# Second routed experts: gate and up of an expert as one load, rows laid out by partition

## The reference, cut to what matters

```python
# hidden_states: [4, 512, 512] -> x: [2048, 512]; w13: [8, 704, 512]; w2: [8, 512, 352]
probs = jax.nn.softmax(router_logits.astype(jnp.float32), axis=-1)
routing_weights, selected_experts = jax.lax.top_k(probs, TOP_K)      # TOP_K = 2
combined = jnp.zeros(x.shape, dtype=jnp.float32)
for e in range(E):                                                   # E = 8
    w_e = jnp.where(selected_experts == e, routing_weights, 0.0).sum(-1)
    h = _silu_and_mul(x @ w13[e].T) @ w2[e].T    # gate: first 352 columns, up: last 352
    combined = combined + w_e[:, None] * h.astype(jnp.float32)
out = shared + combined.astype(x.dtype)
```

## Time and profile before

| what | us |
|---|---|
| runs | 2451.46 median of 3 (2451.32 to 2454.49) |
| profiled execution, its own time | 2455.11 |
| its span in the profile | 2453.5 |
| busy: TensorE | 1960.5 (80%) |
| busy: VectorE | 1437.5 (59%) |
| busy: GpSimd | 1038.2 (42%) |
| busy: ScalarE | 896.1 (37%) |
| mean granted clock of TensorE, share of full speed | 0.917 |

### The profile page before, as it was taken

One profiled execution on the slowest core, in us unless ns is written; L12 is line 12 of the kernel. 1 busy time (PEld: TensorE's weight loads), 2 busy tenths in 40 slices (PEclk: granted clock), 3 DMA queues, 4 the chain that ended last, 5 costly groups with the idle time before them and its releaser, 6 DMA issues. The chain is left out here.

```text
span 2453.5 us, 22106 instructions
## 1 busy us (share of the span) xinstructions
PE 1960.5 (80%) x5587; PEld 956.0 (39%) x5587; DVE 1437.5 (59%) x2046; ACT 896.1 (37%) x1461; POOL 1038.2 (42%) x944
## 2 busy tenths in 40 slices
PE   7367786886886648888888873999999998989990
PEld 2122332332343213333333332666666654555550
DVE  5699888888962649999899975333332331111113
ACT  4455454555521345666466630111111111222220
POOL 0377666666730228888788862010000050000005
PEclk9588898899988769999999996999999999999995
DMA  6403012021001654655747435010000038888886
GB/s 219 191 0 137 1 43 113 0 85 70 5 13 62 239 203 154 241 212 182 262 158 296 167 115 212 20 43 9 26 9 9 9 146 290 301 302 307 298 275 214
DMA packets 159159, 345.77 MB, mean 141 GB/s; under 512 B 14944, under 2 KB 54880, under 8 KB 150368
## 3 DMA queue, kind: packets, MB, share of 16 engines
q1 hardware_dynamic: 146992, 305.23, 34.7%
q0 software_dynamic: 12080, 39.59, 4.7%
HBM read 286.06 MB, written 58.72 MB: 141 GB/s over the span
## 5 line engine op out<-in xcount | busy, mean ns | idle before, releaser
L541 POOL TENSOR_TENSOR work<-work,big 128x512 f32<-128x512 f32 x512 | 658.9, 1295 | 194.2 <-DVE bank L594 188.5
L594 DVE TENSOR_TENSOR_SCAN bank<-bank,work 128x512 f32<-128x512 f32 x512 | 624.8, 1221 | 114.8 <-ACT bank L502 55.3
L437 PE MATMUL bank<-work,ident 128*128 128x512 f32 x896 | 507.7, 678 | 210.1 <-DVE work L570 181.4
L502 ACT ACTIVATE bank<-work,An 128x512 f32<-128x512 f32 x512 | 349.3, 690 | 377.1 <-DVE work L570 373.9
L437 PEld LDWEIGHTS bank<-work,ident 128*128 128x128 f32 x896 | 162.4, 205 | 501.9 <-DVE work L570 356.5
L570 DVE TENSOR_TENSOR work<-bank,big 128x512 f32<-128x512 f32 x512 | 343.9, 672 | 4.3 <-PE bank L437 4.2
L1065 PE MATMUL bank<-big,work 128*128 128x352 f32 x1024 | 315.7, 462 | 4.0 <-DMA big<-sdown 3.3
L1065 PEld LDWEIGHTS bank<-big,work 128*128 128x128 f32 x1024 | 191.7, 191 | 105.4 <-issue 6.1
L1581 PE MATMUL bank<-W,work 128*128 128x512 f32 x384 | 193.7, 617 | 2.1 <-ACT work L1657 1.2
L696 DVE SCALAR_TENSOR_TENSOR work<-work,bank 128x352 f32<-128x352 f32 x39 | 20.3, 521 | 272.8 <-ACT work L691 272.8
L1040 PE MATMUL bank<-big,W 128*128 128x512 f32 x352 | 157.0, 595 | 0.6 <-ACT W L983 0.6
(11 more groups left out here) (270 smaller groups left out, 2363.3 us busy)
## 6 DMA issues: line engine op xcount, KB each, us to landing
big<-bc_d SPq DMA_DIRECT2D x64, 1024.0 KB, 6.7
W<-gate SPq DMA_DIRECT2D x24, 1024.0 KB, 5.3
W<-up SPq DMA_DIRECT2D x24, 1024.0 KB, 5.2
W<-down SPq DMA_DIRECT2D x24, 1024.0 KB, 5.6
work<-xs_d SPq DMA_DIRECT2D x63, 256.0 KB, 5.2
W<-gate SPq DMA_DIRECT2D x20, 704.0 KB, 6.3
W<-up SPq DMA_DIRECT2D x20, 704.0 KB, 7.6
Y<-gate SPq DMA_DIRECT2D x19, 704.0 KB, 6.2
```

The costliest lines, as they stand in the source:

```text
L437: nc.tensor.matmul(YS[:, :], ident[:, :], hC[ring[u[0]]], start=v == 0, stop=v == sums - 1).then_inc(sum_done, 1)
L502: nc.scalar.activation(H[i % 4][:, :], delta[j % 2], ACT.Exp, scale=An[:, j, i:i + 1]).then_inc(dA_done, 1)
L541: nc.gpsimd.tensor_tensor(dBu[i % 2], du[j % 2], Bb[:, i, :], ALU.mult).then_inc(dBu_done, 1)
L594: nc.vector.tensor_tensor_scan(H[i % 4][:, :], H[i % 4][:, :], dBu[i % 2], 0.0, ALU.mult, ALU.add).then_inc(scan_done, 1)
```

## The change

On the host, the transposed `w13` (512 rows of 704 floats per expert: gate, then up) is laid out by partition: for partition p the four rows c * 128 + p stand one behind the other, 2816 floats. The first 256 rows of down are laid out the same way (1024 floats a partition), and the last 96 rows become an array of their own. In the kernel, one DMA brings gate and up of a tile (128 x 2816 floats, 11264 bytes per partition in one piece, where each of the two loads had pieces of 352 floats, 1408 bytes), and one brings the first two blocks of down (pieces of 4096 bytes for 2048). What stands where in SBUF is the same as before, and so are the instructions of all other engines. SyncE's wait for the gate matmuls of tile t - 2 falls away; the merged load waits for the up matmuls of tile t - 2. TensorE's waits ahead of gate and ahead of up now both name the merged load's semaphore.

```diff
--- before.py
+++ after.py
@@ -1296,14 +1296,15 @@
             S["y_out"] = [sem(f"e{k}_y_out{q}") for q in range(2)]
             S["hT_part"] = sem(f"e{k}_hT_part")
             S["xn_in"] = [sem(f"e{k}_xn_in{q}") for q in range(2)]
-            wsem = {m: [sem(f"e{k}_{m}_in{q}") for q in range(2)] for m in ("g", "u", "d")}
+            wsem = {m: [sem(f"e{k}_{m}_in{q}") for q in range(2)] for m in ("gu", "d")}
             WS = [wset(k, q) for q in range(2)]
+            flat = [W, Y[:, :, :].rearrange("p t l -> p (t l)")]
             sh_in, sh_added = sem(f"e{k}_shared_in"), sem(f"e{k}_shared_added")
             shared = wk(9)
 
             def w_in(t, q, done):
-                m = done[0]
-                per = {"g": 16, "u": 16, "d": 32}[m]
+                m = "d" if done[0] == "d" else "gu"
+                per = {"gu": 16, "d": 32}[m]
                 return wsem[m][q], (t - q) * (per // 2) + per
 
             S["w_in"] = w_in
@@ -1317,14 +1318,11 @@
                         if not is_last(t, N):
                             at_least(sp, S["xtr_done"], t)
                             sp.dma_start(xn[1 - q], xs_v[t + 1]).then_inc(S["xn_in"][1 - q], 16)
-                        at_least(sp, S["g_done"], t - 1)
-                        sp.dma_start(WS[q][0], w["gate"][e].rearrange("(c p) f -> p c f", p=P)).then_inc(wsem["g"][q], 16)
                         at_least(sp, S["u_done"], t - 1)
-                        sp.dma_start(WS[q][1], w["up"][e].rearrange("(c p) f -> p c f", p=P)).then_inc(wsem["u"][q], 16)
+                        sp.dma_start(flat[q][:, 0:DK * 2 * F], w["gate_up"][e]).then_inc(wsem["gu"][q], 16)
                         at_least(sp, S["d_done"], t - 1)
-                        dv = w["down"][e]
-                        sp.dma_start(WS[q][2][:, 0:full, :], dv[0:full * P, :].rearrange("(c p) n -> p c n", p=P)).then_inc(wsem["d"][q], 16)
-                        sp.dma_start(WS[q][2][0:F - full * P, full, :], dv[full * P:F, :]).then_inc(wsem["d"][q], 16)
+                        sp.dma_start(flat[q][:, DK * 2 * F:DK * 2 * F + full * D], w["down"][e]).then_inc(wsem["d"][q], 16)
+                        sp.dma_start(WS[q][2][0:F - full * P, full, :], w["down_last"][e]).then_inc(wsem["d"][q], 16)
 
                     def load_shared(i):
 
@@ -1916,10 +1914,16 @@
     }
     w13 = a["L1_ffn_w13"].transpose(0, 2, 1)
     F = w13.shape[2] // 2
+    w2 = a["L1_ffn_w2"].transpose(0, 2, 1)
+
+    def by_partition(v):
+        e, r, f = v.shape
+        return v.reshape(e, r // 128, 128, f).transpose(0, 2, 1, 3).reshape(e, 128, -1)
+
     moe1 = {
         "router": give("router1", np.concatenate([a["L1_ffn_gate_w"], a["L1_ffn_shared_gate_w"]]).T),
-        "gate": give("gate1", w13[:, :, :F]), "up": give("up1", w13[:, :, F:]),
-        "down": give("down1", a["L1_ffn_w2"].transpose(0, 2, 1)),
+        "gate_up": give("gate_up1", by_partition(w13)),
+        "down": give("down1", by_partition(w2[:, :256])), "down_last": give("down_last1", w2[:, 256:]),
         "shared_gate_up": give("sgu1", a["L1_ffn_shared_gate_up_w"].T),
         "shared_down": give("sdown1", a["L1_ffn_shared_down_w"].T),
     }
```

## The result

The changed kernel takes 2482.78 us in the median (2480.19 to 2483.54, 4 runs) against 2452.97 for the kernel before (4 runs). The ratio is 1.0119, 95% interval 1.0101 to 1.0136: 1.2% slower, 29.8 us by the medians. The forecast was 0.7% and 2468.0, with 2480 as the upper end. The sign was right, the size was not.

A forecast was written before the change was run, and what follows sets the result against it. TensorE was taken to set the pace, with loads just in time. Cadence 12.4, scatter 2.0 and start 2.1 us summed to 16.5 us, giving 2468.0 us, 0.7% slower, range 2454 to 2480.

The forecast's parts named there:

- That the merge makes TensorE wait, and the sign: Gate matmuls would wait for the whole merged load, in most tiles, making the kernel 0.7% slower.
- L: Time from a burst's beginning to the landing of the load the gate matmuls wait for: 10.12 us after the change.
- The slower cadence: Bursts of loads would overlap less as tiles take longer, taking 0.2 us off the landing time.
- the rows alone: Longer rows of gate and up would move faster, saving 0.38 us per tile's load (bounds 0.16 and 0.61).
- The landing: The merged load would land 7.4 us after its issue (6.8 to 8.0 by the bounds).
- The start: Tile 0's gate matmuls would start 2.1 us later, waiting for up's landing, with nothing to hide it.
- the cadence: Time per tile in the changed stage would rise from 9.216 to 9.56 us, 12.4 us over 36 tiles.
- Scatter: Single late landings in the changed stage, left out by medians, would add 2 us (bounds 0 and 4).
- the prediction's loop: Two tiles take burst to landing, plus 0.12 us to gate start, plus 8.88 to the next burst but one.
- The first: Rival: long rows save nothing and bursts don't relieve each other, 9.85 us a tile, 2479 us; chance 0.15.
- The second: Rival: row saving and burst relief both at their ends (0.61 and 0.6 us), 2455 to 2458 us; chance 0.17.
- The third: Rival: each load holds the queue beyond its bytes, so one fewer shortens the burst, 2448 us; chance 0.12.

The follow-up runs named there:

- wait_both: Kernel before, loads untouched, with TensorE waiting for both gate and up ahead of the gate matmuls: 2477.72 us, ratio 1.0110.
- split_long: Kernel before with the new layout but gate and up still two loads with two semaphores (rows of 5632 B): 2453.19 us, ratio 1.0004.
- gu_early: Changed kernel with the merged load of tile t+1 issued ahead of down of tile t: 2450.81 us, ratio 0.9999.
- merged_rows: Kernel before with gate and up merged into one load, rows left as in memory (2816 B), down unchanged: 2480.37 us, ratio 1.0115.
- wait_odd: Kernel before with the wait for both gate and up on odd tiles only: 2484.25 us, ratio 1.0128.
- second pair: Changed kernel and kernel before, each executed once more unaltered for a second trace: 2476.68 and 2451.20 us.
- hoist: Changed kernel with SyncE reading the two expert numbers before its wait for down's buffer, same DMAs in order: 2471.32 us, ratio 1.0077.
- no_last: Changed kernel without the load of down's last 96 rows (192 KB) after the first two tiles: 2468.42 us, ratio 1.0078.
- no_main: Changed kernel without the load of down's first 256 rows (512 KB) after the first two tiles: 2466.12 us, ratio 1.0065.
- before_early: Kernel before with gate and up, still two loads of 1408 B rows, issued ahead of down: 2452.48 us, ratio 0.9997.

## Why the prediction was right or wrong

**That the merge makes TensorE wait, and the sign**: right, and shown by wait_both, which has the wait and nothing else, and from the other side by split_long and gu_early.

**L**: forecast 10.12, measured 10.16 and 10.36. The slower cadence took 0.27 us off it (0.20 forecast). Merge and rows together took 0.16, where 0.38 was forecast for the rows alone (bounds 0.16 and 0.61). The landing was forecast at 7.4 us after the issue and is 7.6 and 7.3. In the page Perfetto Trace Analysis of the Trainium skill, section DMA Optimizations, larger DMAs are said to use memory better; its figure for small ones is under 2 KB. The 1408 B rows are below it, and making them longer was worth little: 0.05 us of some 10 by merged_rows against the changed kernel, 0.17 of gate's 8.9 by split_long, whose rows have 5632 B. The same section says that smaller DMAs may let part of the work start sooner, and that is the half of it that decides here.

**The start**: forecast 2.1 us, measured 0.2: from the first x load's issue to the first gate matmul it is 2035.75 - 2027.74 = 8.01 us, and was 7.82. In the second pair it is 8.23 and 6.65, 1.6 more. The term took tile 0's up landing from one trace, and that landing scatters: 10.2, 8.5, 9.8 and 8.0 us after the first x load in the four traces in which these loads are the same (the kernel before twice, wait_both, wait_odd). The merged load has 7.9 and 8.1. By tile 2 the changed kernel is 0.1 us ahead in the first pair and 0.8 behind in the second. So this term was too large and hid some of what the next ones lacked.

**The step that failed is the cadence, in two of its terms: "Scatter", 2 us with bounds 0 and 4, and SyncE's own instructions, put at nothing.** Of these the prediction has only the DMA that falls away, "hidden by the 193.3 us in which it waits"; that the wait for down's buffer became an instruction by itself got no term. In the first pair of traces the steady part grew by 24.95 us where 12.4 + 2.0 were forecast:

- the mean of L, as measured, in the prediction's loop: (10.16 + 0.15 + 8.88) / 2 = 9.595, 13.6 us over 9.216. The forecast had 12.4.
- the two chains are not alike. TensorE goes through even and odd tiles in turn, so the later chain paces both. With the even tiles' L of 10.29 and their 0.18 from landing to start the loop is 9.675: 2.9 us more. wait_odd shows this coupling by itself.
- the clock fell in three tiles, 1.76 us each: 5.3 us. I had read "granted clock 1.00" in the steady part and made no term of it. In eight traces of kernels with late loads there are eleven falls (3 and 1 in the two of the changed kernel, 2 in merged_rows, 1 in wait_both, 3 in wait_odd, 1 in hoist, none in no_last and no_main), each behind an idle time of 1.74 to 2.62 us at the gate matmuls; waits of 2.14 and 1.69 us in the changed kernel, and one of 1.89 in its second trace, had none behind them. The section "HAM oscillation — how this bites in real kernels" of the page TensorE: Matmul & The Clock Gate of the Trainium skill tells of a matmul kernel whose waits for DMAs let each next tile start cold; here it was 1 to 3 tiles in 36.
- the burst begins later behind a gate start: 9.01 us in the changed kernel's tiles without a fall, where 8.88 was taken over from the kernel before. Half of 0.13 over 36 tiles is 2.3 us.
- 0.8 us are left to single late landings, which the later chain passes on while early ones give nothing back. Over the 36 bursts as measured, with start = the later of (last start + 9.10) and (burst + L + 0.15) with 9.01 from start to burst and 1.76 for each fall, the sum is 356.5 us in the first trace and 355.0 in the second, where 356.7 and 355.1 were measured.

The later burst can be read from SyncE's instructions. First L1326 of the kernel before, then L1324 of the changed one, with the first and the last start of each kind:

```profile
L1326 SPq MOVE Y<-down x18: 29/29/29, 2054.2 to 2367.5; - x18
L1326 SPq DMA_DIRECT2D Y<-down x18: 372/373/373, 2059.4 to 2373.2; - x18
```

```profile
L1324 SPq FUSED_REGOPS  x37: 37/37/37, 2051.3 to 2408.1; - x37
L1324 SPq MOVE W<-down x19: 29/29/29, 2051.4 to 2408.2; - x19
L1324 SPq DMA_DIRECT2D W<-down x19: 332/333/333, 2051.5 to 2408.2; - x19
```

In the kernel before the register instruction (MOVE) for down's load stands 5 us ahead of the load, and the load itself waits for the down matmuls. In the changed kernel an instruction on registers waits (L1324, FUSED_REGOPS), and only behind it come a second one and the load. The rows of the down matmuls, before and after:

```profile
2148.66 2.84 PE L726 MATMUL bank<-Y,work 128*128 128x512 f32 x6 [0.78 <-ACT work L739]
```

```profile
2116.87 2.84 PE L726 MATMUL bank<-Y,work 128*128 128x512 f32 x6 [0.78 <-ACT work L739]
```

The first ends at 2151.50 and the load is issued at 2151.53, 0.03 us later; the second ends at 2119.71 and the load is issued at 2119.88, 0.17 us later. In the four traces in which the load waits by itself (the kernel before twice, wait_both, wait_odd) it is 8.85 to 8.88 us from a gate start to the burst, falls left out; in the seven others with the order of the kernel before or of the changed one it is 8.99 to 9.02. No run takes this one thing away alone, so its share is read from traces and not shown by an experiment.

The same loop by the later chain, with each kernel's own time from landing to start (0.14 to 0.25), its time from start to burst (8.88 or 9.01) and its falls, gives 9.89 and 9.83 for the changed kernel (measured 9.91 and 9.86), 9.85 for wait_both (9.84), 9.93 for merged_rows (9.94), 9.74 for hoist (9.75), 9.51 for no_last (9.53) and 9.53 for no_main (9.50). What would have mended the forecast is to take the worse of two chains instead of their mean, to price falls of the clock at the 1 to 3 in 36 tiles that these traces have, and to ask which of SyncE's instructions stands behind its wait.

**The rivals.** The first (rows save nothing, 2479) came nearest in time, but only half by its mechanism: the rows did save next to nothing, but the bursts do relieve each other, and L was not 10.70. The second and the third did not come about. The third's fixed cost per load is refuted once more by merged_rows and wait_both: one load fewer took 0.1 us off L there. The section that the prediction names for that cost, Anatomy of one DMA of the page DMA: Bandwidth & Descriptors of the Trainium skill, gives its 2.0 us for DMAs that GpSimd issues; the loads here are SyncE's.

**No gain from a cure.** The expectation for before_early gave the kernel before 3 to 4 us to lose. Its traces have 5.4 and 2.4 (9.22 and 9.13 a tile against 9.07), and the runs show no gain clear of noise.

## What to carry to other kernels

A load's semaphore counts when the last byte is there, so merging two loads puts the deadline of the first on the landing of the second; before merging, compare that landing with the moment at which the first one's reader is ready (here 10.7 against 9.4 us), not with its own. Where buffers alternate, work out each chain by itself and take the later; and if a load has to grow, bring its issue forward, to where its buffer really comes free. Where a wait lets a burst out, look at which instruction carries the wait: what stands between it and the load is not hidden.

## What was not expected of the hardware

Behind waits of 1.74 to 2.62 us ahead of the gate matmuls TensorE's granted clock fell in eleven cases to a mean of 0.74 over the next eight matmuls, so that a wait of 1.8 us cost 3.5; other waits of up to 2.14 us had no fall behind them. The wait on every second tile alone cost no less (1.0128) than the same wait on all of them (1.0110). And two short register instructions between SyncE's wait and its load, 0.14 us together, are paid in the cadence, though SyncE waits for most of the stage.
